# The scan stage: gathers of four steps on column strips, one scan instruction a step, products in pairs

## The chip, the cores and the metric

The kernel runs on one core of one Trainium2 chip. The metric is the time of one execution in device microseconds. TensorE (PE; its weight loads are listed as PEld), VectorE (DVE), ScalarE (ACT), GpSimd (POOL) and the DMA queue of SyncE (SP) run side by side and hand work to one another through semaphores.

## The reference, cut to what matters

Twelve layers follow one another, each added to `x` (32 sequences of 32 tokens, 256 channels). The change is in the eighth, `L2_attn`: a linear recurrence over the 32 tokens of a sequence. Its 16 heads have 16 channels each, so that each head has a state of 16 by 16 numbers a sequence.

```python
vq = x @ vq_w.T
v, q = jnp.split(vq, 2, axis=-1)
k = jax.nn.sigmoid(x @ key_w.T + key_b)
upd = (1.0 - k)[..., :, None] * v[..., None, :]
decay = k[..., :, None]
def combine(c1, c2):
    a1, b1 = c1
    a2, b2 = c2
    return (a1 * a2, b1 * a2 + b2)
_, kv = jax.lax.associative_scan(combine, (decay, upd), axis=1)
h = jnp.einsum('nthd,nthde->nthe', qh, kv).reshape(n, t, HID)
return h @ out_w.T + out_b
```

## The kernel before

The layers are stages that follow one another; `stage_scan` is the eighth, and `stage_moe_capacity` comes behind it. A stage ends when all engines have left it.

`stage_scan` keeps channels on the 128 partitions. The 1024 tokens are two token halves of 512, the 256 channels two chunks of 128 (`CD` = 2), which gives `HALVES` = 4 blocks of 128 channels by 512 tokens (16 sequences of 32). After layer norm, 12 projections give `vT`, `decay` and `qT` for each block, and `dv`, the difference of neighbouring tokens' `v`, split into `dv_hi` and `dv_lo`. A zero column ahead of each sequence makes a block 16 times 33 = 528 columns wide (`STEP` = 33), so that one scan runs over many sequences.

The **loop** has 4 blocks times 16 value channels (`HD` = 16) = 64 steps, numbered `k` = 16`i` + `e`. A step is:

- **PE, `spread_out(k)`** (L2420, L2421): the rows of value channel `e` of each head are spread over the 16 rows of that head. Two halves of 264 columns (`BITS` = 2, `BIT` = 264), each a matmul of `dv_hi` and one of `dv_lo`, each half into its own PSUM bank. `SLOTS` = 3 steps have their banks (6 of the 8).
- **DVE, the scan** (L2535): `state` = (spread + previous) times `decay`, two instructions of 264 columns, one for each half.
- **POOL, the product** (L2393): `product` = `state` times `qT`, one instruction of 512 columns.
- **PE, `gather_in(k)`** (L2432): a matmul with a 128 by 128 matrix of ones and zeros sums the 16 rows of each head and adds the sum to the output's row of PSUM bank `SUM[i % 2]`. It is fp32 and stands in the trace as two records.

Once a block, PE also makes `query_sums(i)` (L2438), DVE makes `own_values(i)` of it (L2507) and, when the block's 16 gathers are done, `results(i)` (L2513), which gives `hT`. When the first token half is through, four output tiles are projected (`project`, L2442) and added to `x` by DVE (`add`, L2517) in the midst of block 2; the other four behind the loop.

Each engine's order is that in which the code is written; nothing is reordered. PE runs the loop with a lag: at turn `k` it issues `spread_out(k)`, then `gather_in(k - LAG)` with `LAG` = 3. `spread_out(k)` waits until the scan of step `k - 3` has left the slot, the scan until POOL has read the state of step `k - RING` (`RING` = 4), the product until the gather of step `k - RING` is done. SP loads the stage's constants and then weights of later stages.

Of the kernel before, what the change touches and what calls it, by code (L numbers as in the profile page):

```python
# [15 lines left out]
P = 128  # L16
# [5 lines left out]
HALF = 512  # L22
# [2282 lines left out]
def stage_scan(core, cw, xw):  # L2305
# [8 lines left out]
    RING = 4  # L2314
    LAG = 3
    EVICT, QSUM, OUT = 4, 6, (8, 10, 12, 14)
    with ExitStack() as ctx:
# [6 lines left out]
        gather = st.sb("gather", [P, HD, P])  # L2324
# [9 lines left out]
        product = st.sb("product", [P, RING, HALF])  # L2334
        spread = product[:, :, :].rearrange("p r (e m) -> p (r e) m", m=P)
# [16 lines left out]
        SPREAD, SUM = [bank[0:2], bank[2:4], bank[4:6]], bank[6:8]  # L2352
# [6 lines left out]
        def by_seq(a):  # L2359
            return a.rearrange("p (b s) -> p b s", s=SEQ)  # L2360

# [15 lines left out]
        def _(pool):  # L2377
# [9 lines left out]
            for i in range(HALVES):  # L2387
                for e in range(HD):
                    k = i * HD + e
                    pool.wait_ge(state_ready, (k + 1) * BITS)  # L2390
                    if k >= RING:
                        pool.wait_ge(gathered, k - RING + 1)
                    nc.gpsimd.tensor_tensor(by_seq(product[:, k % RING, :]), state[:, k % RING, :, 1:STEP], by_seq(qT[:, i, :]),  # L2393
                                            ALU.mult).then_inc(product_ready, 1)

        @block.tensor
        def _(pe):
# [14 lines left out]
            def spread_out(k):  # L2412
# [3 lines left out]
                if k >= SLOTS:  # L2416
                    pe.wait_ge(state_ready, (k - SLOTS + 1) * BITS)
                for g in range(BITS):
                    now, to = slice(g * BIT, (g + 1) * BIT), SPREAD[k % SLOTS][g][:, 0:BIT]
                    nc.tensor.matmul(to, spread_r[:, e, :], dv_hi[:, i, now], start=True, stop=False)  # L2420
                    nc.tensor.matmul(to, spread_r[:, e, :], dv_lo[:, i, now], start=False, stop=True).then_inc(spread_done, 1)  # L2421

            def gather_in(k):
# [24 lines left out]
            for k in range(HALVES * HD + LAG):  # L2448
# [7 lines left out]
                if i == 2 and e in OUT:  # L2456
                    t = OUT.index(e)
# [37 lines left out]
        def _(dve):  # L2495
# [13 lines left out]
            def results(i):  # L2509
                n, c = divmod(i, CD)  # L2510
                dve.wait_ge(gathered, (i + 1) * HD)
# [9 lines left out]
            for k in range(HALVES * HD):  # L2521
# [3 lines left out]
                if e == QSUM + 1:  # L2525
# [1250 lines left out]
```

## Time and profile before

| | us |
|---|---|
| median of 3 runs (lowest, highest) | 1746.91 (1744.55, 1750.09) |
| the profiled execution | 1756.64 |
| its span, first to last instruction | 1754.7 |
| first scan of the loop starts | 1191.07 |
| last scan of the loop ends | 1282.92 |
| first result tile behind the loop starts (L2513) | 1285.39 |

The profile is of one execution; times in its rows count from the span's start. A row of the timeline merges like instructions that run without a gap ("x14") and gives the first one's start and the union of their times. "[0.16 <-DVE scan_state L2535]" is idle time ahead of the instruction and what ended it. An instruction's mean duration contains its fill and its tail, so that two in a row can start closer together than one lasts: the distance between starts is what a stream of them costs. In the rows of TensorE "128*32" is active rows times columns of the array. Over the whole span PE is busy 90%, DVE 60%, ACT 48%, POOL 44%.

### The profile page before, as it was taken

How to read it: one execution, taken by the hardware profiler on the slowest of the kernel's cores; microseconds unless marked ns; L12 is line 12 of the kernel's file. 1: busy time of each engine (PE TensorE's matmuls, PEld its weight loads, DVE VectorE, ACT ScalarE, POOL GpSimd, SP SyncE). 2: the span in 40 equal slices, each digit the busy share in tenths (PEclk: the TensorE clock that was granted, in tenths of full speed). 3: DMA queues.
4: the chain of work that ended last, by engine and by line, in shares of the span. 5: the costliest groups of instructions: out<-in, count | busy, mean ns of one | idle time of the engine just before them, and what ended most of it. 6: DMA issues, size and time to landing. Idle time of an engine off the chain costs nothing. (4 is left out here: it accounts for less than half of the span.)

```text
span 1754.7 us, 37500 instructions
## 1 busy us (share of the span) xinstructions
PE 1587.3 (90%) x13621; PEld 1349.2 (77%) x13621; DVE 1061.1 (60%) x2989; ACT 846.9 (48%) x2434; POOL 773.9 (44%) x926
## 2 busy tenths in 40 slices
PE   7999999988788999988999999999969879749998
PEld 6889998857557999966889888955649834539997
DVE  5887887546866888844766766748961131353332
ACT  5666666445336888842766666640004222204332
POOL 7655665242339999833211111227733411212332
PEclk9999999989998999989999999999989986969999
DMA  8545545210014433303433333345037273861222
GB/s 277 170 163 168 161 153 165 75 67 2 1 27 157 138 129 128 137 19 114 163 118 104 105 126 105 103 131 158 1 105 225 26 215 103 303 206 26 39 38 29
DMA packets 127222, 205.32 MB, mean 117 GB/s; under 512 B 21034, under 2 KB 92362, under 8 KB 126530
## 3 DMA queue, kind: packets, MB, share of 16 engines
q1 hardware_dynamic: 119016, 189.62, 33.0%
q0 software_dynamic: 6720, 8.79, 3.1%
q10 hardware_dynamic: 1306, 4.51, 0.8%
q8 instruction: 112, 1.84, 0.5%
q14 instruction: 68, 0.56, 0.1%
HBM read 162.54 MB, written 41.14 MB: 116 GB/s over the span
## 5 line engine op out<-in xcount | busy, mean ns | idle before, releaser
L921 DVE TENSOR_SCALAR xattn_oT<-banks,xattn_last 128x256 f32<-128x256 f32 x254 | 111.0, 478 | 90.0 <-PE banks L718 89.8
L817 ACT ACTIVATE xattn_probs<-banks,xattn_negmax 128x257 f32<-128x257 f32 x256 | 124.0, 484 | 61.1 <-DVE xattn_negmax L902 61.0
L822 ACT ACTIVATE xattn_probs<-xattn_probs,xattn_rsum 128x257 f32<-128x257 f32 x256 | 131.9, 515 | 1.4 <-DVE xattn_rsum L906 1.4
L1166 POOL TENSOR_SCALAR xattn_probs<-xattn_probs,xattn_rsum 128x257 f32<-128x257 f32 x128 | 119.7, 935 | 21.2 <-DVE xattn_rsum L1421 21.1
L902 DVE TENSOR_REDUCE xattn_negmax<-banks 128x1 f32<-128x257 f32 x256 | 106.5, 416 | 35.1 <-PE banks L688 33.6
L911 DVE TENSOR_TENSOR xattn_probsT_lo<-banks,xattn_probsT_hi 128x256 fp32r<-128x256 f32 x256 | 105.1, 410 | 9.8 <-ACT xattn_probsT_hi L828 8.8
L633 POOL COPY ctx_stat<-xattn_mv 128x2 f32<-128x2 f32 x32 | 6.0, 189 | 238.0 <-DVE xattn_mv L935 238.0
L828 ACT CAST xattn_probsT_hi<-banks 128x256 fp32r<-128x256 f32 x256 | 95.6, 374 | 31.6 <-PE banks L695 27.5
L695 PE MATMUL banks<-ident,xattn_probs 128*128 128x128 f32 x512 | 103.8, 285 | 3.2 <-ACT xattn_probs L822 2.7
L684 PE MATMUL banks<-xattn_ctxT,xattn_qk_hi 128*128 128x258 f32 x256 | 93.6, 366 | 0.5 <-DVE xattn_qk L898 0.5
L589 POOL TENSOR_SCALAR xattn_ctxT<-xattn_rawT 128x514 fp32r<-128x514 f32 x32 | 50.0, 1562 | 98.3 <-issue 94.5
L3127 PE MATMUL banks<-moe_xinT,moe_w_now 128*128 128x128 f32 x736 | 88.1, 279 | 0.0
L210 ACT COPY xnT<-banks 128x512 f32<-128x512 f32 x40 | 21.2, 590 | 137.2 <-PE banks L190 137.2
L2393 POOL TENSOR_TENSOR scan_product<-scan_state,scan_qT 128x512 f32<-128x512 f32 x64 | 75.7, 1185 | 26.4 <-DVE scan_state L2535 26.1
L3127 PEld LDWEIGHTS banks<-moe_xinT,moe_w_now 128*128 128x128 f32 x736 | 86.4, 196 | 0.1
L713 PE MATMUL banks<-xattn_probsT_hi,xattn_ctxN 128*128 128x256 f32 x256 | 85.0, 332 | 1.2 <-issue 1.2
L3085 POOL DMA_INDIRECT out_dram<-moe_y_slots,moe_row_u x23 | 36.5, 1585 | 109.9 <-DVE moe_y_slots L3252 107.0
L666 PE MATMUL banks<-xattn_qT,xattn_wk 64*128 64x128 f32 x1024 | 73.3, 283 | 12.8 <-DVE xattn_qT L887 10.0
L3137 PE MATMUL banks<-moe_w,moe_hT 128*128 x368 | 83.1, 379 | 0.0
L2535 DVE TENSOR_TENSOR_SCAN scan_state<-banks,scan_decay 128x264 f32<-128x264 f32 x128 | 81.3, 689 | 1.3
L666 PEld LDWEIGHTS banks<-xattn_qT,xattn_wk 64*128 64x128 f32 x1024 | 62.2, 187 | 22.0 <-issue 12.6
L648 PE MATMUL banks<-xnT,xattn_wq 128*128 128x128 f32 x512 | 70.0, 284 | 6.9 <-ACT xnT L210 4.7
(519 smaller groups left out, 5241.6 us busy)
## 6 DMA issues: line engine op xcount, KB each, us to landing
xattn_ctxT<-ctx_partsT SPq DMA_DIRECT2D x64, 516.0 KB, 4.0
xattn_ctxN<-ctx_partsN SPq DMA_DIRECT2D x64, 384.0 KB, 4.1
ctx_partsT<-xattn_ctxT SPq DMA_DIRECT2D x32, 516.0 KB, 2.7
moe_w<-in_L_ffn_W SPq DMA_DIRECT2D x16, 1024.0 KB, 12.9
ctx_partsN<-xattn_ctxN SPq DMA_DIRECT2D x32, 384.0 KB, 3.6
moecap_w_early<-in_L_ffn_w SPq DMA_DIRECT2D x10, 1024.0 KB, 9.1
xattn_rawN<-in_ctx SPq DMA_DIRECT2D x32, 192.0 KB, 2.7
xattn_raw<-in_ctx SPq DMA_DIRECT2D x32, 192.0 KB, 4.4
```

Source lines behind the costliest of these rows:

```text
L666: mm = nc.tensor.matmul(bank[:, k * P:(k + 1) * P], wk_s[r, h // 2, g % 2 * P:(g % 2 + 1) * P], qT[r, h // 2, :], start=True, stop=True, t ...
L684: nc.tensor.matmul(out, unit(qk1[0]), part(0, 0), start=True, stop=False)
L695: mm = nc.tensor.transpose(TB[n % 2][:, c * P:(c + 1) * P], probs[:, n % RING, c * P:(c + 1) * P], core.ident[:, :])
L713: nc.tensor.matmul(first[:, 0:2 * P], first_hi(c), hi[:, c], start=(c == 0), stop=False)
L817: nc.scalar.activation(probs[:, n % RING, :], SB[n % 2][:, 0:KV], ACT.Exp, bias=negmax[:, n % RING:n % RING + 1], accum_out=psum[:, n % RI ...
L822: nc.scalar.mul(probs[:, n % RING, :], probs[:, n % RING, :], rsum[:, n % RING:n % RING + 1]).then_inc(norm_ready, 1)
L828: nc.scalar.copy(probsT[0][:, n // 2 % PAIRS, :, n % 2, :], TB[n % 2][:, 0:2 * P].rearrange("p (c n) -> p c n", c=2)).then_inc(probsT_hi_r ...
L902: nc.vector.tensor_reduce(negmax[:, n % RING:n % RING + 1], SB[n % 2][:, 0:KV], AX.X, ALU.max, negate=True).then_inc(negmax_ready, 1)
L911: nc.vector.tensor_tensor(lo, TB[n % 2][:, 0:2 * P].rearrange("p (c n) -> p c n", c=2), hi, ALU.subtract).then_inc(probsT_ready, 1)
L921: nc.vector.tensor_scalar(oT[k][:, heads, b, :], by_head(out_banks(n)[k][:, k * 2 * P:(k + 1) * 2 * P]), last[:, k, j * PER_TILE + b:j * P ...
L1166: nc.gpsimd.tensor_scalar(probs[:, n % RING, :], probs[:, n % RING, :], rsum[:, n % RING:n % RING + 1], None, ALU.mult).then_inc(norm_read ...
L3127: mm = nc.tensor.matmul(H[n % 2][k][:, f * P:(f + 1) * P], w1_now[:, c, at:at + P], xinT[:, n % 2, c, :], start=(c == 0), stop=(c == CD - 1))
```

## The change

- **Gathers of four steps.** PE gathers four steps (`QUAD` = 4) at one place: four matmuls with 32 output columns, each on its own column strip of the array (`tile_position=(0, z * SEQ)`) and into its own 32 partitions of the same bank. `gather` shrinks from 128 by 16 by 128 to 128 by 16 by 32. So that the sums of a step land within one strip, the host permutes the channels of `vq_w`, `out_w`, `spread` and `same_head`. `gather_in` for steps `k - 8` to `k - 5` follows `spread_out(k)`, for every fourth `k` (`LAG` = 5).
- **One scan a step.** The two halves lie side by side across the boundary of two banks (columns 248 to 776 of the pair), and DVE scans 528 columns in one instruction. PE signals once a step.
- **Products in pairs.** POOL multiplies two steps in one instruction of 1024 columns (`PAIR` = 2), `qT` being read twice.
- **Rings and places.** `RING` of states 4 to 6, `PRODUCTS` = 8; results at `e` = 7 (was 4), query sums at 9 (was 6), own values at 11 (was 7), and the four projections in the loop at steps 45, 47, 49 and 51 (were 40, 42, 44 and 46).

```diff
-    RING = 4
-    LAG = 3
-    EVICT, QSUM, OUT = 4, 6, (8, 10, 12, 14)
+    RING, PRODUCTS = 6, 8
+    PAIR, QUAD = 2, 4
+    LAG = 5
+    EVICT, QSUM, OWN_AT = 7, 9, 11
+    OUT = [2 * HD + o for o in (13, 15, 17, 19)]
@@ POOL
-                    pool.wait_ge(state_ready, (k + 1) * BITS)
-                    if k >= RING:
-                        pool.wait_ge(gathered, k - RING + 1)
-                    nc.gpsimd.tensor_tensor(by_seq(product[:, k % RING, :]), state[:, k % RING, :, 1:STEP], by_seq(qT[:, i, :]),
-                                            ALU.mult).then_inc(product_ready, 1)
+            for k in range(0, HALVES * HD, PAIR):
+                pool.wait_ge(state_ready, k + PAIR)
+                if k >= PRODUCTS:
+                    pool.wait_ge(gathered, (k - PRODUCTS) // QUAD + 1)
+                now, to = slice(k % RING, k % RING + PAIR), slice(k % PRODUCTS, k % PRODUCTS + PAIR)
+                query = by_seq(qT[:, k // HD, :]).unsqueeze(1).broadcast_to([P, PAIR, OWN, SEQ])
+                nc.gpsimd.tensor_tensor(product[:, to, :].rearrange("p r (b s) -> p r b s", s=SEQ), state[:, now, :, 1:STEP], query,
+                                        ALU.mult).then_inc(product_ready, 1)
@@ PE
-                    pe.wait_ge(state_ready, (k - SLOTS + 1) * BITS)
+                    pe.wait_ge(state_ready, k - SLOTS + 1)
...
-                pe.wait_ge(product_ready, k + 1)
-                nc.tensor.matmul(SUM[i % 2], gather[:, e, :], product[:, k % RING, :], start=(e == 0),
-                                 stop=(e == HD - 1)).then_inc(gathered, 1)
+                pe.wait_ge(product_ready, (k + QUAD) // PAIR)
+                for z in range(QUAD):
+                    mm = nc.tensor.matmul(SUM[i % 2][z * SEQ:(z + 1) * SEQ, :], gather[:, e + z, :], product[:, (k + z) % PRODUCTS, :],
+                                          start=(e == 0), stop=(e == HD - QUAD), tile_position=(0, z * SEQ))
+                mm.then_inc(gathered, 1)
...
-                if k >= LAG:
-                    gather_in(k - LAG)
+                if k >= LAG and (k - LAG) % QUAD == QUAD - 1:
+                    gather_in(k - LAG - QUAD + 1)
@@ DVE
                 if k >= RING:
-                    dve.wait_ge(product_ready, k - RING + 1)
-                for g in range(BITS):
-                    dve.wait_ge(spread_done, k * BITS + g + 1)
...
+                    dve.wait_ge(product_ready, (k - RING) // PAIR + 1)
+                dve.wait_ge(spread_done, k + 1)
+                nc.vector.tensor_tensor_scan(flat(state[:, k % RING, :, :]), SPREAD[k % SLOTS], flat(decay[:, i, :, :]), 0.0,
+                                             ALU.add, ALU.mult).then_inc(state_ready, 1)
```

What stands in a row on PE, first in the kernel before, steps 6 to 8 of block 0 with the query sums between:

```order
L2432 MATMUL banks<-scan_product,scan_gather 128x512
L2438 MATMUL banks<-scan_qT,scan_same_head 128x512
L2420 MATMUL banks<-scan_dv_hi,scan_spread_r 128x264
L2421 MATMUL banks<-scan_dv_lo,scan_spread_r 128x264
L2420 MATMUL banks<-scan_dv_hi,scan_spread_r 128x264
L2421 MATMUL banks<-scan_dv_lo,scan_spread_r 128x264
L2432 MATMUL banks<-scan_product,scan_gather 128x512
```

The same engine in the changed kernel, steps 8 to 10 of block 0 (L2427 and L2428 are the spread, L2441 the gather, L2448 the query sums):

```order
L2427 MATMUL banks<-scan_dv_hi,scan_spread_r 128x264
L2428 MATMUL banks<-scan_dv_lo,scan_spread_r 128x264
L2441 MATMUL banks<-scan_product,scan_gather 32x512 x4
L2427 MATMUL banks<-scan_dv_hi,scan_spread_r 128x264
L2428 MATMUL banks<-scan_dv_lo,scan_spread_r 128x264
L2427 MATMUL banks<-scan_dv_hi,scan_spread_r 128x264
L2428 MATMUL banks<-scan_dv_lo,scan_spread_r 128x264
L2448 MATMUL banks<-scan_qT,scan_same_head 128x512
```

Behind every spread of four matmuls stood a gather; now four spreads follow one another and then come the four strips together.

On DVE, blocks 0 and 1 of the loop before (L2507 own values, L2513 results):

```order
L2535 SCALAR_TENSOR_TENSOR scan_state<-banks,scan_decay 128x264 x14
L2507 TENSOR_TENSOR scan_own_v<-banks,scan_vT 128x512
L2535 SCALAR_TENSOR_TENSOR scan_state<-banks,scan_decay 128x264 x26
L2513 TENSOR_TENSOR scan_hT<-banks,scan_own_v 128x512
L2535 SCALAR_TENSOR_TENSOR scan_state<-banks,scan_decay 128x264 x6
```

and in the changed kernel:

```order
L2542 SCALAR_TENSOR_TENSOR scan_state<-banks,scan_decay 128x528 x11
L2517 TENSOR_TENSOR scan_own_v<-banks,scan_vT 128x512
L2542 SCALAR_TENSOR_TENSOR scan_state<-banks,scan_decay 128x528 x12
L2523 TENSOR_TENSOR scan_hT<-banks,scan_own_v 128x512
L2542 SCALAR_TENSOR_TENSOR scan_state<-banks,scan_decay 128x528 x4
```

The scans are half as many and twice as wide, and own values and results stand some steps later. POOL's 64 products of 128x512 become 32 of 128x1024 at the same place.

## Rows read from the trace of the kernel before

**Rows 1.** Windows view: span, each engine's busy time (instructions), clock, DMA share, GB/s.
```profile
1215.00:1240.00 25.00, 25.00 (x111) 15.87 (x110) 24.03 (x39) 0.00 (x0) 21.27 (x18) 1.00 0.00 1
```

**Rows 2.** Timeline, PE and weight loads, one step: start us, us, engine, line, operation.
```profile
1231.45 0.19 PEld L2421 LDWEIGHTS banks<-scan_dv_lo,scan_spread_r 128*128 128x128 f32 x1 [0.24 <-issue]
...
1231.93 1.02 PE L2432 MATMUL banks<-scan_product,scan_gather 128*128 128x512 f32 x2
...
1232.79 0.19 PEld L2421 LDWEIGHTS banks<-scan_dv_lo,scan_spread_r 128*128 128x128 f32 x1 [0.24 <-issue]
```

**Rows 3.** Groups, loop alone: line engine op shapes xcount | busy us, mean ns | idle.
```profile
L2535 DVE TENSOR_TENSOR_SCAN scan_state<-banks,scan_decay 128x264 f32<-128x264 f32 x128 | 81.3, 689 | 1.3
L2393 POOL TENSOR_TENSOR scan_product<-scan_state,scan_qT 128x512 f32<-128x512 f32 x64 | 75.7, 1185 | 26.4 <-DVE scan_state L2535 26.1
```

**Rows 4.** Timeline of DVE in the loop.
```profile
1191.07 3.09 DVE L2535 TENSOR_TENSOR_SCAN scan_state<-banks,scan_decay 128x264 f32<-128x264 f32 x5
...
1199.83 0.69 DVE L2507 TENSOR_TENSOR scan_own_v<-banks,scan_vT 128x512 f32<-128x512 f32 x1 [0.29 <-PE banks L2438]
1200.43 17.13 DVE L2535 TENSOR_TENSOR_SCAN scan_state<-banks,scan_decay 128x264 f32<-128x264 f32 x26
1217.48 0.67 DVE L2513 TENSOR_TENSOR scan_hT<-banks,scan_own_v 128x512 f32<-128x512 f32 x1
1218.06 3.69 DVE L2535 TENSOR_TENSOR_SCAN scan_state<-banks,scan_decay 128x264 f32<-128x264 f32 x6
...
1248.21 0.42 DVE L2517 TENSOR_TENSOR x<-x,banks 128x256 f32<-128x256 f32 x1 [0.47 <-PE banks L2442]
1248.55 2.63 DVE L2535 TENSOR_TENSOR_SCAN scan_state<-banks,scan_decay 128x264 f32<-128x264 f32 x4
...
1271.13 11.79 DVE L2535 TENSOR_TENSOR_SCAN scan_state<-banks,scan_decay 128x264 f32<-128x264 f32 x18
```

**Rows 5.** Timeline of POOL: seven products without a wait, and one of the steady stretch.
```profile
1192.54 8.27 POOL L2393 TENSOR_TENSOR scan_product<-scan_state,scan_qT 128x512 f32<-128x512 f32 x7 [10.54 <-DVE scan_state L2535]
...
1230.64 1.19 POOL L2393 TENSOR_TENSOR scan_product<-scan_state,scan_qT 128x512 f32<-128x512 f32 x1 [0.16 <-DVE scan_state L2535]
```

**Rows 6.** Groups of POOL: the widest fp32 product or sum that it makes.
```profile
L1860 POOL TENSOR_TENSOR attn_x_plus<-x,xn 128x2048 f32<-128x2048 f32 x1 | 4.5, 4510 | 0.6 <-DVE xn L155 0.6
```

**Rows 7.** Timeline of PE in a later stage whose matmuls run on column strips.
```profile
1444.87 0.66 PE L3444 MATMUL banks<-xattn_T,xattn_qk 128*32 128x257 f32 x8
1445.33 0.64 PE L3445 MATMUL banks<-xattn_T,xattn_qk 66*32 66x257 f32 x8
1445.90 0.44 PE L3453 MATMUL banks<-ident,xattn_probs 128*128 128x128 f32 x2
...
1446.39 0.27 PE L3481 MATMUL banks<-ident,xattn_o_norm 128*64 128x128 f32 x1
1446.60 0.86 PE L3469 MATMUL banks<-xattn_N,xattn_probsT 128*32 128x194 f32 x16
```

**Rows 8.** Timeline of the loop's tail: last product, last gather, first result.
```profile
1283.00 1.18 POOL L2393 TENSOR_TENSOR scan_product<-scan_state,scan_qT 128x512 f32<-128x512 f32 x1 [0.17 <-DVE scan_state L2535]
...
1284.23 0.30 PEld L2432 LDWEIGHTS banks<-scan_product,scan_gather 128*128 128x128 f32 x2 [0.73 <-POOL scan_product L2393]
1285.39 0.69 DVE L2513 TENSOR_TENSOR scan_hT<-banks,scan_own_v 128x512 f32<-128x512 f32 x1 [2.47 <-PE banks L2432]
```

**Rows 9.** Windows view of other stages, for TensorE's clock (columns as in Rows 1).
```profile
451.00:452.00 1.00, 1.00 (x3) 0.50 (x3) 0.97 (x2) 0.00 (x0) 0.00 (x0) 0.50 0.00 0
...
453.00:454.00 1.00, 1.00 (x5) 0.60 (x4) 0.96 (x2) 0.99 (x2) 0.92 (x2) 1.00 0.00 0
1540.00:1550.00 10.00, 6.13 (x35) 2.69 (x34) 6.85 (x26) 2.15 (x4) 2.63 (x4) 1.00 1.03 340
1470.00:1480.00 10.00, 8.77 (x49) 5.00 (x45) 1.95 (x7) 2.63 (x6) 0.00 (x0) 0.67 0.00 0
```

More of the change, by code:

```diff
@@ L2323, in stage_scan @@
         bo = st.sb("bo", [P, D])
-        gather = st.sb("gather", [P, HD, P])
+        gather = st.sb("gather", [P, HD, SEQ])
         same_head = st.sb("same_head", [P, P])
@@ L2333, in stage_scan @@
         state = st.sb("state", [P, RING, OWN, STEP])
-        product = st.sb("product", [P, RING, HALF])
-        spread = product[:, :, :].rearrange("p r (e m) -> p (r e) m", m=P)
+        product = st.sb("product", [P, PRODUCTS, HALF])
+        spread = product[:, 0:HD * P // HALF, :].rearrange("p r (e m) -> p (r e) m", m=P)
         hT = st.sb("hT", [P, CD, TOKENS])
@@ L2351, in stage_scan @@
         bank = [b[:, :] for b in core.bank]
-        SPREAD, SUM = [bank[0:2], bank[2:4], bank[4:6]], bank[6:8]
+        SPREAD = [core.banks[:, k * BITS:(k + 1) * BITS, :].rearrange("p g n -> p (g n)")[:, HALF - BIT:HALF + BIT] for k in range(SLOTS)]
+        SUM = bank[6:8]
         PROJ = [(kind, n, c) for n in range(2) for c in range(CD) for kind in ("v", "k", "q")]
@@ L2416, in spread_out @@
                 if k >= SLOTS:
[L2417 removed]
+                    pe.wait_ge(state_ready, k - SLOTS + 1)
                 for g in range(BITS):
[L2419 removed]
+                    now = slice(g * BIT, (g + 1) * BIT)
+                    to = SPREAD[k % SLOTS][:, now]
                     nc.tensor.matmul(to, spread_r[:, e, :], dv_hi[:, i, now], start=True, stop=False)
[L2421 removed]
+                    mm = nc.tensor.matmul(to, spread_r[:, e, :], dv_lo[:, i, now], start=False, stop=True)
+                mm.then_inc(spread_done, 1)
             def gather_in(k):
@@ L3747 @@
     same_head = p[:, None] // HD == p[None, :] // HD
-    spread = same_head[:, None, :] & (p[:, None, None] % HD == np.arange(HD)[None, :, None])
-    data["spread"] = np.ascontiguousarray(spread, dtype=np.float32)
-    data["same_head"] = np.ascontiguousarray(same_head, dtype=np.float32)
-    data["gather"] = np.ascontiguousarray(spread.transpose(2, 1, 0), dtype=np.float32)
+    strip, place = p // SEQ, p % SEQ
+    at = place % (P // HD) * HD + place // (P // HD) * 4 + strip
+    chunks = np.concatenate([at, P + at])
+    vq = data["L2_attn_vq_w_T"]
+    data["L2_attn_vq_w_T"] = np.ascontiguousarray(np.concatenate([vq[:, 0:D][:, chunks], vq[:, D:]], axis=1))
+    data["L2_attn_out_w_T"] = np.ascontiguousarray(data["L2_attn_out_w_T"][chunks])
+    spread = same_head[:, None, :] & (p[:, None, None] % HD == np.arange(HD)[None, :, None])
+    data["spread"] = np.ascontiguousarray(spread[at], dtype=np.float32)
+    data["same_head"] = np.ascontiguousarray(same_head[:, at], dtype=np.float32)
+    own = np.stack([(at[e % 4 * SEQ:(e % 4 + 1) * SEQ] % HD == e)[None, :] & same_head[:, at[e % 4 * SEQ:(e % 4 + 1) * SEQ]]
+                    for e in range(HD)], axis=1)
+    data["gather"] = np.ascontiguousarray(own, dtype=np.float32)
     data["number"] = np.arange(512, dtype=np.float32)
```

21 lines of the change are left out of this document (8 added, 13 removed).

## The prediction, made before the changed kernel ran

> **What bounds the kernel now.** I went from the page (which stages the change touches) to the windows view of the loop, then to the timeline of each engine in it. The stages follow one another, and the change touches only the scan stage, so its price is read there: from the first scan at 1191.07 to the last one's end at 1271.13 + 11.79 = 1282.92, 91.85 us, and the tail up to the first result at 1285.39 [rows 4, 8]. Within the loop the windows view shows PE busy 25.00 of 25 us, DVE 24.03 and POOL 21.27 [rows 1]; busy time alone doesn't say which one sets the pace. The starts do. On PE one whole step lies between 1231.45 and 1232.79: 1.34 us, of which 0.48 is the spread (1231.45 to 1231.93) and 0.86 the gather (1231.93 to 1232.79), and there is no wait in it [rows 2]. On DVE, five scans at the loop's head, when PE is ahead, take 3.09 us; with the last one's full 0.69 taken off, the four distances between starts are 0.60 each [rows 3, 4]. The six scans from 1218.06 (3.69 us) give the same 0.60, with POOL busy beside them. The 26 scans from 1200.43 take 17.13, so (17.13 - 0.69) / 25 = 0.66: there DVE is held up by PE a little before each scan, too little to be listed as idle. So a step costs DVE 1.20, PE 1.34. POOL, where it has a backlog, makes a product every (8.27 - 1.19) / 6 = 1.18 us, and elsewhere waits 0.16 for the scan [rows 5]. **PE sets the pace at 1.34; DVE is next at 1.20, POOL at 1.18.** All three must fall for the loop to fall much.
>
> **PE, the gathers.** Four gathers cost 4 x 0.86 = 3.44 us. Four strips together are to be read from a later stage: eight records of 257 columns on strips of 32 (four matmuls, two records each) take from 1444.87 to 1445.33, 0.46 us [rows 7]. Our own 512 columns took 0.86 in one full matmul, so 257 columns one after the other would be 4 x 0.43 = 1.72. The strips do run side by side, at 0.46 / 0.43 = 1.07 of a single one. A gather of four steps is then 0.92. Turning to strips and back is bounded by the same rows: the full matmul at 1446.39 (128 columns, 0.11) is followed by strips at 1446.60, 0.10 more than it needs; the eight at 1445.33 take 0.57 up to the full matmul at 1445.90, 0.11 over 0.46, and I take 0.14. So four steps cost PE 4 x 0.48 + 0.92 + 0.24 = 3.08 us instead of 5.38: 0.77 a step. Bounds: 0.69 (strips and turns free) to 1.40 (strips one after another). I take 0.77 because the row is the same engine, type and strip width.
>
> About this the Trainium skill ("TensorE: Matmul & The Clock Gate", Part 3, Measured speedup vs the span model) states 2.38 times for three column tiles of 512 columns, not 3. By an estimate from that figure, four strips of our width would take 0.86 x 3 / 2.38 = 1.08, the loop's body would be the same and its tail 0.16 us longer. The row above, 1.07 of a single matmul for four, speaks against it.
>
> **DVE, one scan.** Its other operations of 512 columns (own values, 1199.83 to 1200.43) stand 0.60 apart and those of 256 columns (1248.21 to 1248.55) 0.34 [rows 4]: 0.26 per 256 columns, 1.02 ns a column, and 0.07 that is fixed. The scan, with 264 columns in 0.60, needs (0.60 - 0.07) / 264 = 2.0 ns a column, twice theirs; at exactly twice, 0.54 to 0.55 are columns and the rest is fixed. The fixed part is 0.05 to 0.07, and joining two scans saves it once: a step is 1.15 (bounds 1.13, and 1.20 if a read across two banks costs what the joint saves, above that only if it stalls, for which no row speaks). Sum: 64 x 1.15 = 73.7. DVE's other work in the loop is unchanged: four own values at 0.60, three results at 0.58 (1217.48 to 1218.06), four sums at 0.34: 5.5. **Loop 79.2, plus 0.08 for the last one's tail: the last scan ends at 1270.4, 12.5 us earlier.**
>
> **POOL, products in pairs.** 512 columns take 1.185, 2048 take 4.51 in another stage [rows 3, 6]: (4.51 - 1.185) / 1536 = 2.16 ns a column, and a pair takes 1.185 + 512 x 2.16 ns = 2.29. Bounds: 2.25 to 2.37 (twice the present one). DVE offers a pair every 2.30, so POOL keeps up or falls behind by at most 0.07 a pair, which DVE's 5.5 us of other work gives back: 32 x 2.37 = 75.8 is under 79.2. It costs the path nothing in the loop, but it is now nearly as late as DVE.
>
> **Do the batches wait for one another?** Let the scan of step k-5 end at T. Spread k starts when the scan of k-3 has left the slot, T + 2.30 + 0.07, and ends at T + 2.85. The pair (k-6, k-5) is multiplied from T + 0.16 to T + 2.45, so the gather doesn't wait for it. Gather and turns end at T + 4.01, spread k+1 at T + 4.49, readable 0.30 later (that is what lies between the last gather, 1284.23 + 0.86, and 1285.39 [rows 8]). DVE wants it at T + 5 x 1.15 = T + 5.75: 0.96 us to spare in every group of four. The queue behind PE's new wait for products holds the next spreads; the slack covers it as long as a product isn't late by more than 1.3 us. The moved projections and query sums never share a turn with a gather except step 9's neighbour, 8; each adds 0.86 to PE once, and PE has 4 x 1.15 - 3.08 = 1.5 us spare in each group. In the kernel before, the four sums waited about 0.5 each for PE and the own values 0.3 to 0.5 [rows 4]; those waits go, and are within the 12.5.
>
> **The tail.** The last product is now a pair (2.29 instead of 1.18: +1.11) and the last gather 0.92 with the turn of 0.10 instead of 0.86: +0.16. Behind it nothing changes. +1.25 with rounding. The three edits of constants (a gather matrix of a quarter of its size, permuted weights) lie beside the projections and cost nothing; if they mattered they would be a gain.
>
> **Sum.** 12.5 - 1.25 = 11.3 us. The profiled execution would go from 1756.64 to 1745.3; it lies 9.7 over the median of the runs. From the median: 1746.91 - 11.3 = **1735.6**.
>
> **Rivals.**
> 1. *POOL becomes the bound.* If the pair of three-part access with qT read twice costs more than width alone, from about 79.2 / 32 = 2.48 a pair the loop follows POOL. At 2.65: 32 x 2.65 = 84.8, some 5.5 lost, 1741. For: POOL already has only 0.01 spare. Against: the product before reads the same rows of 32 out of 33 at 1.185.
> 2. *The joint saves nothing.* Step 1.20, loop +3.3: 1738.9.
> 3. *The batches ping-pong*, 0.3 us of DVE idle in each of 16 groups: 4.8, 1740.4.
> 4. *The other side: the clock.* PE is busy without a break today; then it idles a third of each group. The clock has fallen to its half level (1.2 GHz) where work was thin: 0.67 on average in a stretch with PE busy 8.77 of 10 us, while another with 6.13 kept 1.00 [rows 9]. At the low level four steps cost PE 2 x 3.08 = 6.2, 1.54 a step: PE is the bound again, the loop 98.6, and query sums and projections (8 x 1.71 = 13.7) add to it: 112 against 91.85, 1768. Each us at the low level costs 1 - 1.15 / 1.54 = 0.25, so it loses the whole gain only if it lasts over 45 of the 80 us. Against: at the low level PE would have no gap, and where PE had none the clock came back, 0.50 at 451 and 1.00 at 453 [rows 9].
> 5. *The strips don't overlap here.* Four steps then cost PE 1.92 + 3.44 + 0.24 = 5.6, 1.40 a step, and the four gathers in a row (3.7 us) outlast the slack above: some 1.5 a step, about 1760. Rows 7 speak against it.
> 6. *POOL far slower*: a pair over 79.2 / 32 + 11.3 / 32 = 2.83 gives a time above today's.
>
> On rival 4 the Trainium skill ("TensorE: Matmul & The Clock Gate", A second HAM failure mode: psum-queue depth-cycling) states that a TensorE that idles briefly between groups of matmuls can swing between the two clock levels. The row with 6.13 busy at 1.00 does not show that, the row with 0.67 does.
>
> **Chances.** The forecast 0.64; rival 1 0.11; rival 2 0.07; rival 3 0.08; rival 4 0.04; rivals 5 and 6 0.03 each. The forecast's own spread is 1732.5 (fixed part 0.07, pair 2.25) to 1738; the range for 8 in 10 takes in rivals 2 and 3 and most of rival 1: 1732 to 1743. A measurement tells 0.3%, 5.2 us. Faster by more: the forecast, rivals 2 and 3 and half of rival 1, 0.83; slower by more: rivals 4, 5 and 6 less some overlap with no change, 0.08; within it the rest, 0.09.
>
> **What would show it.** Scans of 528 columns of about 1.23 us, 1.15 apart; products of 1024 columns at 2.29 with a wait of 0.0 to 0.2 before them; four strips of the gather in 0.92; PE idle in every group and its clock at 1.00 from 1191 to 1270; last scan ending at 1270.4. The prediction is wrong where DVE's idle time in the loop is over 1 us, a pair is over 2.48, or a clock of 0.50 stands in the loop. If the loop is as forecast and the time is not, the cause lies behind the stage.

## The result, and the profile of the changed kernel

The changed kernel takes **1738.42 us** (median of 5 runs, 1733.68 to 1740.48), the kernel before 1746.91 (5 runs, 1744.55 to 1750.09). The ratio is 0.9947, with a 95% interval of 0.9927 to 0.9967: faster by some 9 us. The forecast was 1735.6, with a range of 1732 to 1743. The profiled execution took 1740.48, its span is 1738.6. It is 16.2 us shorter than the profiled one before (1756.64); the scan stage accounts for 9.4 of that, the other 6.7 lie in stages whose code is the same.

Read in the order of the prediction, first the windows view of the changed kernel, the stretch that answers to [rows 1] (span, busy us and instructions of PE, weight loads, DVE, ACT, POOL; granted clock, DMA share, GB/s):

```profile
1215.00:1240.00 25.00, 20.66 (x131) 12.70 (x128) 25.00 (x24) 0.00 (x0) 22.47 (x11) 1.00 0.00 1
```

DVE and PE have changed places: DVE is busy 25.00 of 25, PE 20.66. That DVE sets the pace is read from its groups in the loop, 1192 to 1271 (line, engine, operation, names, shapes, count | busy us, mean ns | idle before, and what ended it), against [rows 3]:

```profile
L2542 DVE TENSOR_TENSOR_SCAN scan_state<-banks,scan_decay 128x528 f32<-128x528 f32 x64 | 74.7, 1234 | 0.0
L2399 POOL TENSOR_TENSOR scan_product<-scan_state,scan_qT 128x1024 f32<-128x1024 f32 x31 | 67.8, 2187 | 22.7 <-DVE scan_state L2542 20.7
L2427 PE MATMUL banks<-scan_dv_hi,scan_spread_r 128*128 128x264 f32 x124 | 39.6, 341 | 12.3 <-DVE scan_state L2542 12.3
```

The 64 scans have no idle time before them; PE now waits 12.3 us for scans, and POOL 20.7. The starts say it too, in the timelines of DVE and POOL (start us, us, then as above; in brackets the idle time before), against [rows 4, 5]:

```profile
1192.00 12.72 DVE L2542 TENSOR_TENSOR_SCAN scan_state<-banks,scan_decay 128x528 f32<-128x528 f32 x11
1204.64 0.67 DVE L2517 TENSOR_TENSOR scan_own_v<-banks,scan_vT 128x512 f32<-128x512 f32 x1
1205.22 13.88 DVE L2542 TENSOR_TENSOR_SCAN scan_state<-banks,scan_decay 128x528 f32<-128x528 f32 x12
```

```profile
1226.12 13.66 POOL L2399 TENSOR_TENSOR scan_product<-scan_state,scan_qT 128x1024 f32<-128x1024 f32 x6 [0.70 <-DVE scan_state L2542]
```

Eleven scans in 12.72 us stand (12.72 - 1.23) / 10 = 1.15 apart, twelve in 13.88 the same. Six pairs of products stand (13.66 - 2.19) / 5 = 2.29 apart, which is DVE's 2 x 1.15. The loop runs from 1192.00 to 1269.84 + 1.23 = 1271.07: **79.07 us, where 91.85 stood before and 79.3 was forecast.**

PE over one group of four, in its timeline, against [rows 2] (matmuls alone; each record's own length overlaps the next, so the starts count):

```profile
1229.13 1.06 PE L2441 MATMUL banks<-scan_product,scan_gather 128*32 128x512 f32 x8
1230.12 0.39 PE L2427 MATMUL banks<-scan_dv_hi,scan_spread_r 128*128 128x264 f32 x1
...
1230.72 0.35 PE L2427 MATMUL banks<-scan_dv_hi,scan_spread_r 128*128 128x264 f32 x1
...
1231.83 0.39 PE L2427 MATMUL banks<-scan_dv_hi,scan_spread_r 128*128 128x264 f32 x1 [0.39 <-DVE scan_state L2542]
```

The four strips of a gather and the turn back take 1229.13 to 1230.12, 0.99 us, where four full gathers took 4 x 0.86 = 3.44. That is 3.5 times. The 2.38 for three tiles that the Trainium skill ("TensorE: Matmul & The Clock Gate", Part 3, Measured speedup vs the span model) states would have made it 1.08 and the turns on top; the trace is nearer to strips that run wholly side by side. One thing was not foreseen: the spread behind a gather or a pause takes up to 0.60 (1230.12 to 1230.72) and not 0.48. PE's own work for four steps is thus 3.4 us (four spreads of 0.59, 0.60, 0.59 and 0.56 from 1224.87 on, 0.09 ahead of the gather, and 0.99) and not 3.08; it is still under DVE's 4.60.

The tail is where the forecast gave way. Timeline of all engines behind the last scan, and the windows view of the same stretch of the changed kernel, against [rows 8]:

```profile
1273.36 0.20 PEld L2441 LDWEIGHTS banks<-scan_product,scan_gather 128*32 128x32 f32 x8 [4.41 <-POOL scan_product L2399]
1273.37 1.94 PE L2441 MATMUL banks<-scan_product,scan_gather 128*32 128x512 f32 x8 [3.50 <-POOL scan_product L2399]
1275.37 0.69 DVE L2523 TENSOR_TENSOR scan_hT<-banks,scan_own_v 128x512 f32<-128x512 f32 x1 [4.30 <-PE banks L2441]
...
1278.23 0.42 DVE L2527 TENSOR_TENSOR x<-x,banks 128x256 f32<-128x256 f32 x1 [2.16 <-PE banks L2452]
1279.71 0.42 DVE L2527 TENSOR_TENSOR x<-x,banks 128x256 f32<-128x256 f32 x1 [1.06 <-PE banks L2452]
...
1282.18 1.08 DVE L142 BATCH_NORM_STATS2 moecap_ln_stats<-x 128x6 f32<-128x256 f32 x3 [0.32 <-PEq L2319]
```

```profile
1271.00:1282.00 11.00, 7.22 (x24) 4.27 (x24) 2.45 (x6) 0.00 (x0) 2.19 (x2) 0.69 0.00 0
```

And the same place of the kernel before, in its timeline of DVE:

```profile
1285.39 0.69 DVE L2513 TENSOR_TENSOR scan_hT<-banks,scan_own_v 128x512 f32<-128x512 f32 x1 [2.47 <-PE banks L2432]
1287.31 0.42 DVE L2517 TENSOR_TENSOR x<-x,banks 128x256 f32<-128x256 f32 x1 [1.22 <-PE banks L2442]
...
1290.64 0.75 DVE L142 BATCH_NORM_STATS2 moecap_ln_stats<-x 128x6 f32<-128x256 f32 x2 [0.32 <-PEq L2317]
```

PE waits 3.50 us for the last pair product. The granted clock averages 0.69 in the window: in windows of half a microsecond it falls to 0.50, the lower of the two levels (1.2 GHz), at 1272.5, still within that wait, and is back at 1.00 from 1279.3. The last eight strip matmuls take 1.94 instead of 1.06. The tail (last scan's end to the first result) is 4.30 instead of 2.47, and from the first result to the next stage's first instruction 1275.37 to 1282.18 = 6.81 pass instead of 1285.39 to 1290.64 = 5.25. The stage as a whole (its first instruction at 1162.1, at 1161.1 before) is 120.10 us against 129.50, 9.4 shorter, made of -12.8 in the loop, +1.8 in the tail and +1.6 behind it.

### The profile page after: what moved, and what is told of

It reads as the page before. It is cut to its first block and busy times, and to the rows that moved or that the text cites. A ratio compares the mean times of both kernels' runs of the same rounds, so it can differ in the third digit from the quotient of the medians.

```text
span 1738.6 us, 37370 instructions
## 1 busy us (share of the span) xinstructions
PE 1554.9 (89%) x13621; PEld 1328.6 (76%) x13621; DVE 1052.8 (61%) x2925; ACT 846.9 (49%) x2434; POOL 766.9 (44%) x894
## 5 line engine op out<-in xcount | busy, mean ns | idle before, releaser
L666 PE MATMUL banks<-xattn_qT,xattn_wk 64*128 64x128 f32 x1024 | 73.3, 283 | 12.8 <-DVE xattn_qT L887 10.0
L2399 POOL TENSOR_TENSOR scan_product<-scan_state,scan_qT 128x1024 f32<-128x1024 f32 x32 | 70.0, 2186 | 22.8 <-DVE scan_state L2542 20.7
L666 PEld LDWEIGHTS banks<-xattn_qT,xattn_wk 64*128 64x128 f32 x1024 | 62.2, 187 | 22.0 <-issue 12.6
L3178 ACT ACTIVATE moe_hT<-banks,moe_b_now 128x128 f32<-128x128 f32 x184 | 52.6, 368 | 47.2 <-PE banks L3134 47.1
```

Source lines behind the costliest of these rows:

```text
L666: mm = nc.tensor.matmul(bank[:, k * P:(k + 1) * P], wk_s[r, h // 2, g % 2 * P:(g % 2 + 1) * P], qT[r, h // 2, :], start=True, stop=True, t ...
```

## The experiments

Times of whole runs say little here: executions of one kernel lie up to 24 us apart (1727.31 to 1750.95 for one of them), and their mean granted clock goes with it (0.961 for the lowest, 0.949 for the highest). Within the scan stage the profiles repeat to a few hundredths of a microsecond where the clock stays up. So each experiment was read by its stage, in one table. "Idle" is DVE's listed waiting for PE within the loop, "tail" runs from the last scan's end to the last block's result, "behind" is from the last block's result (its hT) to the next stage. The ratio is to the kernel before on the same chip.

| kernel | loop | idle | tail | behind | ratio, 95% interval |
|---|---|---|---|---|---|
| before | 91.85 | 3.90 | 2.47 | 5.25 | |
| changed | 79.07 | 0 | 4.30 | 6.81 | 0.9947, 0.9927 to 0.9967 |
| changed, again | 79.08 | 0 | 4.29 | 8.30 | 0.9975, 0.9954 to 0.9996 |
| strips only | 84.39 | 1.94 | 2.44 | 6.86 | 0.9990, 0.9969 to 1.0010 |
| joined scan only | 92.00 | 3.16 | 2.47 | 5.24 | 0.9997, 0.9972 to 1.0022 |
| two scans | 82.92 | 0.52 | 3.42 | 8.20 | 0.9994, 0.9976 to 1.0011 |
| single products | 80.97 | 1.50 | 3.23 | 7.33 | 0.9973, 0.9949 to 0.9997 |
| full gathers | 97.67 | 16.3 | 6.04 | 5.24 | 1.0070, 1.0047 to 1.0093 |
| PE 0.96 later a group | 82.03 | 1.63 | 4.30 | 8.22 | one execution, 1735.82 us |
| PE 1.44 later a group | 86.67 | 5.41 | 3.43 | 8.13 | one execution, 1737.72 us |
| extra matmuls, tail | 80.98 | 1.49 | 3.49 | 5.25 | 0.9949, 0.9931 to 0.9966 |
| extra, head and tail | 79.08 | 0 | 3.49 | 5.25 | 0.9941, 0.9921 to 0.9961 |
| the same, single products | 79.08 | 0 | 2.44 | 5.25 | 0.9942, 0.9921 to 0.9963 |

### One part at a time

The strips alone: the changed kernel with two scans a step and products of one step.

```diff
-    PAIR, QUAD = 2, 4
+    PAIR, QUAD = 1, 4
...
-                nc.vector.tensor_tensor_scan(flat(state[:, k % RING, :, :]), SPREAD[k % SLOTS], ...)
+                for g in range(BITS):
+                    scan = nc.vector.tensor_tensor_scan(flat(state[:, k % RING, of, :]), SPREAD[k % SLOTS][:, g * BIT:(g + 1) * BIT], ...)
```

> Of the changed kernel, only the gathers on strips with their rings and places; two scans a step and single products as before. Theory (the pace is set by the slowest of three engines: PE 1.34, DVE 1.20, POOL 1.18 us a step before): DVE is the bound at 1.20 a step, loop from first scan to end of last 64 x 1.204 + 5.5 + 0.1 = 82.7 us against 91.85 before and 79.07 in the changed kernel, so the strips alone carry 9.2 of 12.8 us. Tail (last scan's end to first result) 3.2 to 3.5. Whole time 9 us under before, +-3. Rival (the parts only work together, because DVE and POOL were nearly as late as PE): DVE and POOL hold each other up, loop 86 us or more, DVE idle over 2 us.

The loop took 84.39, but 1.94 of it are waits that the kernel before doesn't have. They stand in DVE's timeline, and the windows view shows the clock there (0.63) and in the steady stretch (1.00):

```profile
1197.21 1.30 DVE L2544 TENSOR_TENSOR_SCAN scan_state<-banks,scan_decay 128x264 f32<-128x264 f32 x2 [0.87 <-PE banks L2428]
1198.98 1.31 DVE L2544 TENSOR_TENSOR_SCAN scan_state<-banks,scan_decay 128x264 f32<-128x264 f32 x2 [0.47 <-PE banks L2428]
...
1208.65 7.28 DVE L2544 TENSOR_TENSOR_SCAN scan_state<-banks,scan_decay 128x264 f32<-128x264 f32 x12 [0.60 <-PE banks L2428]
```

```profile
1192.00:1200.00 8.00, 8.00 (x38) 4.89 (x41) 6.67 (x12) 0.00 (x0) 6.72 (x6) 0.63 0.79 162
1212.00:1237.00 25.00, 19.99 (x123) 11.83 (x122) 25.00 (x43) 0.00 (x0) 23.60 (x21) 1.00 0.00 1
```

Without them the loop is 82.45, close to the 82.7 expected for a step of 1.20. So the strips lift PE's bound, and DVE's two scans are the next one. The rest of the expectation missed: the tail is 2.44 where 3.2 to 3.5 were expected, and the whole time, expected 9 us under the kernel before, was 4 under it by the medians and can't be told from it; the stage is 5.9 shorter.

The joined scan alone: the kernel before with one scan of 528 columns a step, and nothing else.

> The kernel before with one thing changed: one scan of 528 columns a step (across the bank boundary), full gathers a step, single products, old rings and places. Theory: PE still needs 1.34 a step, so the loop stays at 91 to 92.5 us and the whole time within 2 us of before, though DVE's busy time falls to about 79 us. Rival (DVE, busy 24.0 of 25 us, was the bound): the loop falls by 64 x 0.05 = 3 us or more, to 88.5.

The loop stayed at 92.00: nothing gained, as it must be when PE sets the pace. Its groups show PE without waits and DVE waiting in PE's place:

```profile
L2536 DVE TENSOR_TENSOR_SCAN scan_state<-banks,scan_decay 128x528 f32<-128x528 f32 x64 | 79.2, 1251 | 4.1
...
L2435 PE MATMUL banks<-scan_product,scan_gather 128*128 128x512 f32 x128 | 65.2, 593 | 0.7 <-POOL scan_product L2394 0.6
```

The changed kernel with two scans a step (the second part of the diff above alone):

> The changed kernel with two scans of 264 columns a step again, all else kept. Theory: a step costs DVE 1.20 instead of 1.15, loop 64 x 0.052 = 3.3 us longer than the changed kernel's 79.07: 82.4, DVE idle under 0.5 us. Rival (POOL's pairs would be the bound as soon as DVE is not): a loop under 81.

82.92 with 0.52 of idle time, so 82.40. Against the 79.07 of the joined scan that is 3.33 / 64 = 0.052 us a step. Steady rows of the two traces give 0.048: twelve steps take 14.36 us here (1202.97 to 1217.33) and 13.79 in the changed kernel (1205.22 to 1219.01); the rest was lost around the wait. That is the fixed part of one scan less whatever the read across the border of two banks costs. With the 0.05 to 0.07 that [rows 4] gave for the fixed part, the border costs 0.02 us at most.

The changed kernel with products of one step (the first part of the diff alone):

> The changed kernel with 64 products of 512 columns instead of 32 of 1024, all else kept. Theory: POOL makes a product every 1.18 to 1.19 us, a little slower than DVE's 1.15, falls behind by 0.04 a step and gets it back in DVE's other work (5.5 us): loop 79.1 +-0.4; the tail is about 1.0 us shorter than the changed kernel's 4.30, as one product of 1.18 stands behind the last scan instead of a pair of 2.19. So the pairs give nothing, and the whole time is 0 to 2 us under the changed kernel. Rival (pairs are what lets POOL keep up): POOL sets the pace at 1.19 to 1.35 with its wait of 0.16, loop 80.5 to 86 us, time over the changed kernel's.

DVE waited twice, 0.79 and 0.71 us, each time behind a fall of the clock, as its timeline and the windows around the waits show (0.66, 0.83; between them 1.00):

```profile
1193.95 2.60 DVE L2542 TENSOR_TENSOR_SCAN scan_state<-banks,scan_decay 128x528 f32<-128x528 f32 x2 [0.79 <-PE banks L2428]
...
1224.30 7.00 DVE L2542 TENSOR_TENSOR_SCAN scan_state<-banks,scan_decay 128x528 f32<-128x528 f32 x6 [0.71 <-PE banks L2428]
```

```profile
1186.00:1196.00 10.00, 9.56 (x42) 6.40 (x42) 9.12 (x9) 0.00 (x0) 9.18 (x9) 0.66 0.79 170
1196.00:1216.00 20.00, 16.37 (x104) 9.79 (x106) 20.00 (x19) 0.00 (x0) 18.73 (x17) 1.00 0.00 1
1218.00:1228.00 10.00, 8.72 (x49) 5.17 (x49) 9.29 (x9) 0.00 (x0) 9.23 (x9) 0.83 0.01 2
```

The loop of 80.97 lies in the range of the rival (80.5 to 86), but what DVE waited for is PE, not POOL. Without the waits the loop is 79.47, 0.4 over the changed kernel's. Whether that remainder was the single products' or the clock's is settled below, where a kernel with single products and a steady clock takes 79.08: **the pairs bring the loop nothing**.

### Do the strips pay because they run side by side?

The changed kernel, with each group's gathers as four full matmuls in a row (with the full gather matrix and the old order of the weights; the output's bias lies in `hT` to make room):

```diff
-                    mm = nc.tensor.matmul(SUM[i % 2][z * SEQ:(z + 1) * SEQ, :], gather[:, e + z, :], product[:, (k + z) % PRODUCTS, :],
-                                          start=(e == 0), stop=(e == HD - QUAD), tile_position=(0, z * SEQ))
+                    mm = nc.tensor.matmul(SUM[i % 2], gather[:, e + z, :], product[:, (k + z) % PRODUCTS, :],
+                                          start=(e + z == 0), stop=(e + z == HD - 1))
```

> The changed kernel (one scan a step, products in pairs, gathers held back for groups of four steps), but each gather is four full 128x128 fp32 matmuls one after the other into one 128x512 sum, as before, with before's gather matrix and before's order of the weights. Theory (the loop got shorter because the four strips run side by side): TensorE needs 4 x 0.48 + 4 x 0.86 = 5.36 us for four steps, and since three spread slots don't outlast four gathers in a row VectorE waits in each group: 1.34 to 1.5 a step, loop 88 to 98, TensorE the bound, 9 to 19 us more than the changed kernel's 79.1, and no gain over before. Rival (the gain is from handling gathers, products and scans in batches, whatever the gathers' width): loop below 84.

The loop took 97.67, longer than before's, and the kernel is 0.7% slower than before. The timelines of PE and of DVE:

```profile
1226.51 3.59 PE L2441 MATMUL banks<-scan_product,scan_gather 128*128 128x512 f32 x8
1229.54 0.69 PE L2427 MATMUL banks<-scan_dv_hi,scan_spread_r 128*128 128x264 f32 x1
...
1232.10 0.36 PE L2427 MATMUL banks<-scan_dv_hi,scan_spread_r 128*128 128x264 f32 x1 [0.55 <-DVE scan_state L2542]
...
1232.67 3.60 PE L2441 MATMUL banks<-scan_product,scan_gather 128*128 128x512 f32 x8
```

```profile
1230.70 4.70 DVE L2542 TENSOR_TENSOR_SCAN scan_state<-banks,scan_decay 128x528 f32<-128x528 f32 x4 [0.74 <-PE banks L2428]
1236.86 1.26 DVE L2542 TENSOR_TENSOR_SCAN scan_state<-banks,scan_decay 128x528 f32<-128x528 f32 x1 [1.46 <-PE banks L2428]
```

A group of four takes 1226.51 to 1232.67, 6.16 us, 1.54 a step. DVE runs dry while PE gathers, and then PE waits 0.55 for a slot that DVE has had no time to free. Working in batches is a loss by itself (the stage takes 138.87 us where 129.50 stood before); it is the strips' 0.99 in place of 3.44 that makes it a gain. The prediction's rival 5 had this price: some 1.5 a step and about 1760; measured were 1.54 in this group, 1.53 over the loop (97.67 / 64), and 1757.67.

### How much slack is in a group of four?

The prediction worked out 0.96 us between the end of the spread behind a gather and the scan that wants it. Here PE is made late on purpose, in that spread alone (in the second kernel `7` in place of `5`):

```diff
             def spread_out(k):
                 i, e = divmod(k, HD)
+                times = 5 if k > LAG and (k - 1 - LAG) % QUAD == QUAD - 1 else 1
...
-                    nc.tensor.matmul(to, spread_r[:, e, :], dv_hi[:, i, now], start=True, stop=False)
+                    for r in range(times):
+                        nc.tensor.matmul(to, spread_r[:, e, :], dv_hi[:, i, now], start=True, stop=r < times - 1)
```

> The changed kernel, with TensorE made later on purpose once in every group of four steps: in the spread right behind a gather the first of its matmuls is issued four times more for each half (8 more of 128x264 at 0.12 us, 0.96 us in all; the sums are the same since each starts the bank anew). It measures the slack of a group of four, worked out in the prediction as 0.96 us. Theory (slack about 0.96): VectorE waits for nothing or up to 0.1 us a group, loop 79.1 to 80.5. Rival 3 (the groups already touch one another, slack 0.3 or less): 0.6 us of VectorE's waiting a group, loop 87 or more. If the pace were set by TensorE's sum alone (3.08 + 0.96 = 4.04 of 4.6): 79.1.

> The same with six more for each half: 12 more matmuls of 0.12, 1.44 us later once in every group of four. Theory (slack about 0.96): VectorE waits 1.44 - 0.96 = 0.48 us in each of some 14 groups, loop 79.1 + 6.7 = 85 to 87. Rival (only the sum on TensorE counts, 3.08 + 1.44 = 4.52 of VectorE's 4.6): loop 79.1 to 79.6. Rival 3 (slack 0.3 or less): over 1.1 a group, loop 94 or more.

The loops took 82.03, over the 80.5 that was the most expected, and 86.67, as expected. Four scans of an ordinary group in the first kernel's timeline of DVE, and in the second's:

```profile
1224.60 4.92 DVE L2544 TENSOR_TENSOR_SCAN scan_state<-banks,scan_decay 128x528 f32<-128x528 f32 x4
...
1230.02 4.69 DVE L2544 TENSOR_TENSOR_SCAN scan_state<-banks,scan_decay 128x528 f32<-128x528 f32 x4
```

```profile
1226.32 4.70 DVE L2544 TENSOR_TENSOR_SCAN scan_state<-banks,scan_decay 128x528 f32<-128x528 f32 x4 [0.67 <-PE banks L2430]
1231.65 2.40 DVE L2544 TENSOR_TENSOR_SCAN scan_state<-banks,scan_decay 128x528 f32<-128x528 f32 x2 [0.63 <-PE banks L2430]
...
1248.93 1.26 DVE L2544 TENSOR_TENSOR_SCAN scan_state<-banks,scan_decay 128x528 f32<-128x528 f32 x1 [1.13 <-PE banks L2430]
```

In the first, four scans without a listed wait take 4.92 where DVE's own other work gives the group air, 4.69: 0.23 late, so 0.96 - 0.23 = 0.73 of slack. In the second, a group takes 1231.65 - 1226.32 = 5.33 where four steps need 4.60: 0.73 late, so 1.44 - 0.73 = 0.71. Both agree on **0.7 us, not 0.96**. The spread before the gather and the one behind it each take some 0.12 more than the 0.48 that was reckoned with, the gather with its turns 0.08 less than its 1.16; that leaves 0.8, and the last 0.1 is not accounted for. Where a projection (L2454 there) falls into the group (1248.93) 1.13 are lost, 0.5 more. The group still has room in the changed kernel, so rival 3 (ping-pong) is excluded. The idea that only PE's sum counts is excluded too: in the first kernel PE's own work is 3.4 + 0.96 = 4.4 us a group, under 4.60, and would have cost nothing.

### The clock, in the tail and at the head

Three kernels with more work for PE, whose sums nobody reads. In the tail:

```diff
+                if k == HALVES * HD + LAG - 1:
+                    pe.wait_ge(own_ready, HALVES)
+                    for _ in range(4):
+                        nc.tensor.matmul(SUM[0], same_head[:, :], qT[:, 3, :], start=True, stop=True)
                 if k >= LAG and (k - LAG) % QUAD == QUAD - 1:
```

and in the second and third also at the loop's head, where the first gather comes only in step 8; the third makes single products, with three matmuls in the tail:

```diff
+                if 1 <= k < LAG + QUAD - 1:
+                    nc.tensor.matmul(SUM[0][:, 0:HALF // 2], same_head[:, :], qT[:, 3, 0:HALF // 2], start=True, stop=True)
```

> The changed kernel with four more fp32 128x512 matmuls on TensorE (same_head by qT of block 3, into the sum bank that nothing reads any more), issued after block 3's own values are read and ahead of the last gather. They compute nothing that is used. In the changed kernel's profile the granted clock fell at 1272.5 for 6.8 us while TensorE waited 4.4 us for the last pair product; the tail was 4.30 us (scan end to hT of block 3) and 6.81 us more passed to the next stage's first instruction, against 2.47 and 5.24 in the kernel before. Theory (TensorE's idling in the tail brings the clock down, and the half clock stretches the last gather and the last projections): with TensorE busy there the clock stays at 1.00 to the stage's end, the tail is 2.19 + 0.37 of single work of the pair + 1.06 + 0.7 = 3.5 to 3.9 us, and the stretch behind it 5.2 to 5.4; together 2 us less than in the changed kernel, some 0.1% of the time, less than a comparison of whole times can show. Rival (the stretch behind the tail is longer because of the order of the last adds or of hT's two halves, not because of the clock): the clock stays up and the stretch still takes 6.8. Loop: as the changed kernel, 79.1, in either.

> The kernel with the four tail matmuls and, in steps 1 to 7 of the scan loop, where no gather has begun yet, one more fp32 128x256 matmul a step into the first sum bank (0.43 us each by half of a 128x512 one, so TensorE has 0.91 of each 1.15 us there instead of 0.48). They compute nothing that is used. Theory (the dips of the granted clock at the loop's head come from TensorE having little to do before the first gather, and each costs VectorE 0.5 to 0.9 us of waiting): no dip between the first scan and the tenth, loop 79.1 in every execution, VectorE without idle time in the loop; stage 2 to 3 us shorter than the changed kernel's mean, 1736 to 1738 in all where the changed kernel gives 1738. Rival (the dips follow from what TensorE did in the stage's head, ahead of the loop, which this leaves alone): a dip at the loop's head stays and the loop is 79.6 to 81.

> The kernel with the extra matmuls at the loop's head and three in the tail, but the product made one step at a time (PAIR = 1) instead of two. Theory: Vector paces the loop either way, so the loop is the same 79.1 to 79.4; the tail has one 1.19 us product in place of the 2.19 us pair behind the last scan, so 2.5 to 2.7 us, and the stretch behind it 5.2 to 5.4: 1 us less than the kernel with pairs and the same matmuls. Rival (single products at 1185 ns plus 0.07 between them are too slow for scans 1.15 apart: GpSimd becomes the bound): scans 1.25 apart in long rows and the loop 80.5 or more with VectorE idle on product_ready.

> The changed kernel once more, unchanged, beside the three kernels with extra matmuls on the same chip. Theory (the loop's length is set by 64 scans at 1.15 us, and what differs from one execution to the next is where the granted clock falls): loop 79.1 with no dip inside it or 79.6 to 80.6 with one, VectorE's idle time in the loop accounting for the whole difference; tail 3.4 to 4.3 by whether the last gather meets the low clock. The time is 0.993 to 0.998 of the kernel before's. Rival (the 79.07 of the first profile was a lucky one and the joint costs more as a rule): loop above 80.6 with no idle time on VectorE, scans further apart than 1.16.

The timeline of DVE behind the last scan in the kernel with both and pairs, its windows view there (granted clock 1.00), and then the timeline in the kernel with single products:

```profile
1269.88 0.69 DVE L2529 TENSOR_TENSOR scan_hT<-banks,scan_own_v 128x512 f32<-128x512 f32 x1 [3.49 <-PE banks L2441]
1271.79 0.42 DVE L2533 TENSOR_TENSOR x<-x,banks 128x256 f32<-128x256 f32 x1 [1.22 <-PE banks L2452]
```

```profile
1266.00:1276.00 10.00, 7.92 (x34) 4.26 (x33) 3.64 (x9) 0.00 (x0) 2.52 (x2) 1.00 0.00 0
```

```profile
1264.97 0.69 DVE L2529 TENSOR_TENSOR scan_hT<-banks,scan_own_v 128x512 f32<-128x512 f32 x1 [2.44 <-PE banks L2441]
```

With PE busy in the tail the clock stayed at 1.00 there in three profiles of three; in the seven profiles with strips and without that work it fell in all seven, in the second half of PE's wait of 2.9 to 3.7 us or up to 1.7 us behind it. With full gathers PE waits only 1.54 us there, and the clock stayed at 1.00. With PE kept busy the tail is 3.49 with pairs, and the stretch behind it 5.25, as before. The rival, that the order of the last adds makes that stretch longer, is out: the order is the same. So PE's wait for the last product is what brings the clock down, and with pairs tail and stretch behind it then take 11.1 to 12.6 against 8.7: a cost of **2.4 to 3.9 us**. Where the fall came behind the last gather (strips only, two scans, PE 1.44 later), the tail itself was not stretched (2.44, 3.42, 3.43) and the whole loss is behind it. The single product takes another 1.05 off the tail.

The head is less clear. Without extra work there the clock fell inside the loop in four profiles of the nine with gathers in groups of four (strips only, two scans, single products, and extra matmuls in the tail alone), with it in none of two. That fits the theory and doesn't show it. Nor were all falls at the head: in three of the four profiles a second one came later, 19 us into the loop with the strips only and 38 us into it in the other two. The windows view of the kernel with extra matmuls in the tail alone:

```profile
1190.00:1210.00 20.00, 16.82 (x93) 11.04 (x92) 18.89 (x18) 0.13 (x1) 14.30 (x7) 0.83 0.67 182
1226.00:1236.00 10.00, 8.76 (x49) 5.25 (x49) 9.37 (x9) 0.00 (x0) 8.77 (x5) 0.83 0.01 2
```

What a fall inside the loop costs is shown: DVE's listed waits are 0.52 for 3.4 us at the low level, and 1.49 to 1.94 for 10.2 us, 0.15 to 0.19 for each. Waits too small to be listed come on top: the two loops of 80.98 and 80.97 are 1.9 longer than the same loops without a fall (79.08), 0.19 for each of 10.2 us.

The changed kernel, run again, repeats its loop (79.08) and its tail (4.29), and no profile shows the joint itself costing more. But 79.07 is not what every execution gets: up to the tail the kernel with extra matmuls in the tail is the same code, and of the three profiles of this code two took 79.1 and one 80.98. What decides whether the clock falls there stays open. The last kernel's stage, 116.68 us, is 3.4 shorter than the changed kernel's and its median 1733.83, the lowest of all. Its ratio to the kernel before, 0.9942, can't be told from the changed kernel's own two, 0.9947 and 0.9975.

## Why the prediction was right, and where it was off

**What bounds the kernel.** PE's 1.34 a step was the pace: joining the scans alone gained nothing (92.00), strips alone gained what PE had over DVE (82.45 without the listed waits). Both joined give 79.07.

**PE's gather, 0.92 and turns of 0.24.** Measured 0.99 with the turn back and 0.09 ahead of it, 1.08 for 1.16. Against that stood up to 0.12 more for each spread behind a pause or a gather, so that four steps cost PE 3.4 and not 3.08. PE had room, so neither moved the loop.

**DVE's step, 1.15.** Measured 1.15, the joint's saving 0.05. The sum of 64 scans and 5.5 us of other work came out at 79.07 for 79.3.

**POOL's pair, 2.29, bounds 2.25 to 2.37.** Measured 2.187, below the lower bound: the slope from the 2048-column row was too steep for it. Rival 1 would have needed 2.48. In the loop POOL waits for DVE, so the error cost nothing, and made the tail 0.1 shorter than reckoned.

**Slack of a group, 0.96.** 0.7, by the two kernels that are late on purpose. The conclusion held, with less to spare.

**The tail, +1.25.** This is the term that failed. Its mechanism, a pair in place of one product, is right: with the clock up the tail grows by 3.42 - 2.47 = 0.95 (two scans) to 3.49 - 2.47 = 1.02 (with the extra matmuls). Left out was that PE waits 3.5 us in it and the clock falls to the low level. "Behind it nothing changes" is the sentence that was wrong: +1.83 in the tail and +1.57 behind it, 3.4 instead of 1.25.

**The clock, rival 4.** It was priced as a loss of the whole loop, with a chance of 0.04, and that didn't come. Its mechanism did, in small: the clock fell in all seven profiles in which PE waited 2.9 to 3.7 us in the tail, and inside the loop in some, and came back each time. One of the latter is of the changed kernel's own loop code, with DVE idle for 1.49 us; by the prediction's own signs (a clock of 0.50 in the loop, DVE idle over 1 us) that execution was a miss. The reason against it (at the low level PE has no gap) explains the return, not that there would be no falls. The price of 0.25 us for each at the low level was too high; 0.19 was measured by the length of the loop. DVE's listed waits come late in a fall: with single products the clock fell at 1186.6 and DVE ran on until its one wait ended at 1193.95. That fits slots filled ahead, which was not tested by itself. The Trainium skill ("TensorE: Matmul & The Clock Gate", A second HAM failure mode: psum-queue depth-cycling) describes such swings between groups of matmuls; the windows with 0.66 and 0.83 above agree, while the loop of the changed kernel's own two profiles, with PE idle in every group, kept 1.00.

**The total.** Stage -9.4 in the profiles where -11.3 was forecast; medians 1746.91 - 1738.42 = 8.5. The two agree within what can be told. The medians of the other comparisons gave 4.6 us for the same kernel. The same code outside the scan stage takes 1603.9 to 1619.8 us in the profiles of the changed kernel and its variants (span less stage), and that spread is larger than the gain; the forecast's 3 us of error in all can't be split further by whole times. The range held because it took in terms of this size, not because the clock in the tail was seen.

## What to carry to other kernels

Find the pace from distances between starts, engine by engine, and change all that are near it at once: a scan joined alone was worth nothing, and with the strips some 3 us. Work held back for a batch needs the batch to be cheap as well as rare: the same batches with full gathers made the stage 9.4 us longer than before. Where a change gives TensorE pauses, look at the granted clock right behind them, above all where it waits for the last item of another engine. There keep the last items small: a single product in the tail and a few idle matmuls ahead of it took 3.4 us off the stage.

## What the runs showed of the hardware that was not expected

- TensorE's granted clock fell to 0.50, in seven profiles of seven and for 3.4 to 10.2 us, in or just behind a wait of 2.9 to 3.7 us at the end of the loop; three or four matmuls of 128x512 put into that wait kept it at 1.00 in three profiles of three.
- It also fell inside the loop in four profiles of nine, for 3.4 or 10.2 us in all, and of three profiles of the same loop code in one alone.
- A spread (four matmuls of 264 columns) that follows a pause or a gather on strips takes 0.56 to 0.60 us in the changed kernel, in the unbroken row of the kernel before 0.48.
- Four strips of 32 columns, 512 columns wide in fp32, take 0.99 us with the turn back to full width, a single full matmul 0.86.
- A scan that reads across two banks costs almost the same a column as one within a bank: 1.15 for 528 columns, 0.60 for 264, so that joining two saves 0.05.
